# A perceiver layer: keys and queries turned by VectorE in 32x32 blocks, and scores on 16 parts of the array

## What is computed

```python
x = x + xattn(layernorm(x), ctx)      # 16 heads of 32: softmax(q k^T / sqrt(32)) v with k = v = ctx, then @ W_out.T + b_out
x = x + attn(layernorm(x))            # projections, rope, 16 heads over the 32 rows of a batch, then @ Wo + bo
x = x + ffn(layernorm(x))             # softmax gate over 8 experts, argmax; that expert's gelu MLP 512-512-512
```

## Time and profile before

| | us |
|---|---|
| median of 3 runs | 944.97 |
| lowest and highest | 943.59, 949.37 |
| profiled execution | 948.28 |
| its span, first to last instruction | 946.1 |

### The profile page before, as it was taken

The page is one execution under the profiler, slowest core; times in us unless marked ns, Lnnn a source line. Parts: engine busy times, 40 slices in busy tenths (PEclk is TensorE's granted clock), DMA queues, the critical chain, the costliest instruction groups (busy, mean ns, idle before and its releaser), DMA issues.

```text
span 946.1 us, 27317 instructions
## 1 busy us (share of the span) xinstructions
PE 853.3 (90%) x11224; PEld 644.3 (68%) x11224; DVE 523.7 (55%) x1127; ACT 436.3 (46%) x1083; POOL 314.5 (33%) x661
## 2 busy tenths in 40 slices
PE   5997989999999999999999999999976459999998
PEld 3554767767686776868777686777765347777775
DVE  2565456565656656566665656656543343554552
ACT  2444455555645555464555646455532123343332
POOL 2022323233332323232332423233231045666553
PEclk9998999999999999999999999999987569999999
DMA  9512121112212112122212212211050189433330
GB/s 316 185 47 58 46 78 60 58 60 78 69 58 80 57 58 84 55 69 70 68 58 66 82 54 65 77 58 58 2 189 12 42 280 387 130 94 99 111 93 3
DMA packets 40074, 85.40 MB, mean 90 GB/s; under 512 B 9230, under 2 KB 10510, under 8 KB 39952
## 3 DMA queue, kind: packets, MB, share of 16 engines
q1 hardware_dynamic: 34048, 71.58, 23.1%
q0 software_dynamic: 3680, 10.23, 3.2%
q10 hardware_dynamic: 2224, 1.86, 0.7%
HBM read 75.27 MB, written 10.22 MB: 90 GB/s over the span
## 4 chain that ended last, share of the span: by engine, by line
PE 72%; DVE 9%; ACT 8%; issue 6%; POOL 3%; ACTq 1%; DMA 0%; DVEq 0%; POOLq 0%
PE bank L414 9%; PE scores L1351 9%; PE bank L1366 8%; PE bank L416 7%; PE bank L415 7%; PE scores L459 6%; PE bank L472 4%; PE bank L447 4%; PE bank L408 3%; PE bank L485 3%; ACT soft_block L764 3%; ACT prob L717 2%; DVE negmax L919 2%; POOL operand_lo L1156 2%; PE bank L623 2%
## 5 line engine op out<-in xcount | busy, mean ns | idle before, releaser
L717 ACT ACTIVATE prob<-scores,negmax 128x257 f32<-128x257 f32 x256 | 119.3, 472 | 161.9 <-DVE negmax L919 160.9
L919 DVE TENSOR_REDUCE negmax<-scores 128x2 f32<-128x514 f32 x128 | 88.2, 689 | 151.4 <-PE scores L459 151.4
L414 PE MATMUL bank<-qkv_hi,operand_hi 128*128 128x396 f32 x256 | 103.0, 402 | 0.0
L1351 PEld LDWEIGHTS scores<-rows_t,w 128*128 128x128 f32 x736 | 87.7, 196 | 11.6 <-issue 10.5
L415 PE MATMUL bank<-qkv_lo,operand_hi 128*128 128x396 f32 x256 | 88.9, 347 | 0.0
L416 PE MATMUL bank<-qkv_hi,operand_lo 128*128 128x396 f32 x256 | 88.8, 347 | 0.0
L459 PE MATMUL scores<-k_t,q_t 32*32 32x257 f32 x2048 | 86.9, 395 | 1.9 <-ACT prob L717 0.5
L1351 PE MATMUL scores<-rows_t,w 128*128 128x128 f32 x736 | 87.9, 279 | 0.7 <-ACT rows_t L1389 0.7
L447 PE MATMUL bank<-consts,context 128*128 128x128 f32 x512 | 79.7, 279 | 4.5 <-ACT k_t L702 4.4
L1366 PE MATMUL bank<-w_all,hidden 128*128 x184 | 82.8, 592 | 0.0
L472 PE MATMUL bank<-consts,prob 128*128 128x128 f32 x512 | 81.1, 281 | 0.0
(11 more groups left out here) (211 smaller groups left out, 1744.0 us busy)
## 6 DMA issues: line engine op xcount, KB each, us to landing
context<-in_ctx SPq DMA_DIRECT2D x64, 512.0 KB, 3.8
w_all<-in_L_ffn_W SPq DMA_DIRECT2D x16, 1024.0 KB, 8.3
b<-in_L_ffn_b SPq DMA_DIRECT2D x23, 256.0 KB
x_tile<-in_x SPq DMA_DIRECT2D x16, 256.0 KB, 3.8
x_scratch<-x_tile SPq DMA_DIRECT2D x16, 256.0 KB, 2.0
soft_block<-in_L_xattn_W_out SPq DMA_DIRECT2D x1, 1024.0 KB, 12.1
late<-in_L_attn_Wk_r_w SPq DMA_DIRECT2D x1, 1024.0 KB, 14.4
soft_block<-in_L_attn_Wo_w SPq DMA_DIRECT2D x1, 1024.0 KB, 5.1
```

What stands on the lines that cost most here:

```text
L414: pe.matmul(to, op_hi[op][:, c, :], w_hi[name][:, c, columns], start=(c == 0), stop=False)
L717: act.activation(prob[pair][:, gg, :], scores[:, gg, 0:J], ACT.Exp, bias=negmax[b % 2][:, g:g + 1], accum_out=sums[t % 2][:, g, bl:bl + 1] ...
L919: dve.tensor_reduce(negmax[b % 2][:, 2 * pair:2 * pair + 2], scores[:, :, 0:J], AX.X, ALU.max, negate=True).then_inc(maxed, 1)
L1351: done = pe.matmul(scores[:, m // 2, (m % 2) * P:(m % 2 + 1) * P], w1[h * G + k][:, m * P:(m + 1) * P], rows_t[h][:, k, :], start=(k == 0) ...
```

## The change

- Keys: PE's transposes, the copies and POOL's work for the last row go. DVE turns each half of a batch's context (`turn_keys`, two block transposes of 128x512) in 32x32 blocks from SBUF to SBUF, at steps 1 and 3 of the batch before. So a quarter of the context rows stays on each 32 partitions, with a head's channels across them.
- Queries: DVE turns a tile's normed rows once the same way (`turn_queries`). Four DMAs per batch on SP's queue then copy the batch's 32 partitions to each of the four partition quarters (`spread_queries`). The scale goes into the norm's root.
- Scores: one block per batch. 16 matmuls of one column for the 257th row, then 64 matmuls of 64 columns, each on 32 rows and 32 columns of the array: row quarter `r` writes bank `r`, head `hl` its quarter of the output partitions. `scores` has four banks. `largest` is one reduction over 1024 elements and two tiny operations; `exp` reads 256 elements across four banks; `exp_last` makes the last row's probabilities on ACT.
- Banks: of eight, four go to scores, one to probabilities and one to attention, so the tile's stages and the set-up's units have two instead of three.
- Steps: nearly all offsets move, and `move_prob` is ACT's for both pairs.

```diff
+QK = C2 * HD
...
 TILE = BT * STEPS
 (INVERT, PLACE_LAST, PLACE_INV, X_BIAS, SPREAD, SPREAD_INV, ATT, ATT_INV, ATT_HI, ATT_LO, XOUT, X1, SCALE1, TURN1, QKV, OUT_BIAS, TURN_Q, TURN_K,
  SELF, SOFT, SOFT_EXP, SOFT_SUM, SOFT_SCALE, SOFT_TURN, SOFT_PLACE, AV, OUT, X2, SCALE3, TURN3, GATE, CHOOSE, RANK) = (
-    -7, -1, -5, 3, 0, 4, 2, 4, 8, 5, 10, 14, 15, 19, 23, 25, 34, 39, 43, 45, 47, 49, 49, 55, 55, 60, 83, 87, 87, 96, 110, 113, 119)
-
-MEASURE_X, SCALE_X = 2 * STEPS + 6, 2 * STEPS + 10
+    -8, 3, -7, 11, 0, 4, 2, 5, 3, 9, 12, 19, 21, 22, 27, 40, 37, 39, 48, 54, 54, 55, 58, 60, 58, 70, 88, 92, 97, 99, 117, 118, 130)
+
+MEASURE_X, SCALE_X = 2 * STEPS + 1, 2 * STEPS + 6
 LAST_STEP = TILE * T + RANK + 2
 
 
-SCORE_AT = (0, 4)
-TURN_C_AT = (2, 7)
-TURN_P_AT = (5, 10)
-ATTEND_AT = (10, 15)
-KEEP_AT = (4, 10)
-QUERIES_AT = 10
-
-DVE_KEYS = (1,)
-DVE_PROB = (0,)
+
+SCORE_AT = 0
+KEYS_AT = (1, 3)
+TURN_P_AT = (3, 10)
+ATTEND_AT = (6, 11)
+QUERIES_AT = 34
+SPREAD_Q_AT = 0
+
+DVE_PROB = ()
 
 
...
-UNIT_AT = [2, 3, 4, 6, 8, 10, 11, 13, 14, 15, 16, 17, 18, 20, 22, 23, 25, 27, 29, 31, 33, 35, 36, 37, 39]
+UNIT_AT = (2, 4, 4, 6, 6, 8, 9, 9, 14, 16, 17, 17, 17, 21, 22, 24, 25, 25, 25, 30, 35, 35, 36, 37, 42)
...
-    negmax = [sba(f"negmax{i}", [P, G]) for i in range(2)]
+    negmax_256, negmax, last_s = sba("negmax_256", [P, G]), sba("negmax", [P, G]), sba("last_s", [P, G])
...
-    k_t = [sbx(f"k_t{i}", [P, 2, J]) for i in range(2)]
-    prob = [sbx(f"prob{i}", [P, 2, J]) for i in range(2)]
+    k_t = [sbx(f"k_t{i}", [P, C2, D]) for i in range(2)]
+    prob = sbx("prob", [P, G, C2, P])
     prob_t = [sbx(f"prob_t{i}", [P, 2, C2, P]) for i in range(2)]
-    q_t = sbx("q_t", [P, G, BT, S])
+    q_t = sbx("q_t", [P, D])
+    staged_c = sbx("staged_c", [P, G, D])
+    q_all = [sbx("q_all0", [P, D]), staged_c[:, 3, :]]
 
     low_bias = sba("low_bias", [P, G])
     rot_bias = sba("rot_bias", [P, 2, 2, ROPE])
     rot_q, rot_k = sba("rot_q", [P, 2, 2, ROPE]), sba("rot_k", [P, G, 2, ROPE])
...
-    scores = ctx.enter_context(nc.psum_tensor("scores", [P, 2, 512], F32))
-    psum = [ctx.enter_context(nc.psum_tensor(f"bank{i}", [P, 512], F32)) for i in range(6)]
...
         return s_[:, :].unsqueeze(2).broadcast_to([P, H, S])
+
+    def quarter_of(b, r):
+
+        bl = b % BT
+        return q_all[b % 2][r * HD:(r + 1) * HD, :], q_t[bl * HD:(bl + 1) * HD, :]
 
...
-    bank_of = {"spread": 0, "xout": 1, "norm": 2, "qkv0": 0, "qkv2": 0, "out": 0, "inv": 1, "gate": 1, "av": 1, "qkv1": 1, "q": 1, "k": 1, "norm3": 2, "rank": 2, "qkv3": 2, "self": 2}
+    bank_of = {"spread": 1, "xout": 1, "norm": 1, "qkv0": 1, "qkv2": 1, "out": 0, "inv": 0, "gate": 0, "av": 0, "qkv1": 0, "q": 0, "k": 1, "norm3": 0, "rank": 1, "qkv3": 0, "self": 1}
...
 
+        def spread_queries(b):
+
+            until.wait_ge(queries_turned, b // BT + 1)
+            until.wait_ge(scored, b - 1)
+            if b == 1:
+                until.wait_ge(columns_made, ROT_Q)
+            for r in range(4):
+                sp.dma_start(*quarter_of(b, r)).then_inc(queries_spread[b % 2], 16)
+
         def load_x(t):
+            if t >= 2:
+                until.wait_ge(unit_done, UNITS.index(("rot", 0)) + 1)
...
@@ -372,6 +391,8 @@
         for step in range(LAST_STEP):
             b, k = divmod(step, STEPS)
             t, bl = divmod(b, BT)
+            if k == SPREAD_Q_AT and b + 1 < B:
+                spread_queries(b + 1)
             if k == 5 and bl == 1 and t + 1 < T:
...
-        def place_queries(t):
-            until.wait_ge(const_loaded, 16)
-            until.wait_ge(normed_x, t + 1)
-            if t:
-                until.wait_ge(k_moved[1], BT * t + 1)
-            turn(norm_x, context_bank, queries_turned)
-
-        def turn_context(b, pair):
-            until.wait_ge(context_loaded[b % 4], 16 * (b // 4 + 1))
-
-            if pair == 0:
-                until.wait_ge(k_moved[1], b)
-                if b <= 1 or b % BT == 1:
-                    until.wait_ge(queries_placed, b // BT + 1)
-            else:
-                until.wait_ge(k_moved[0], b + 1)
-            for gg in range(2):
-                for c in range(C2):
-                    g = 2 * pair + gg
-                    at = (gg * C2 + c) * P
-                    done = pe.transpose(context_bank[:, at:at + P], context[b % 4][:, c, g * P:(g + 1) * P], ident)
-            done.then_inc(context_turned, 1)
-
-        def score(b, pair):
-            t, bl = divmod(b, BT)
-            until.wait_ge(queries_placed, t + 1)
-            until.wait_ge(k_moved[pair], b + 1)
-            until.wait_ge(k_last_moved, 2 * b + pair + 1)
-            until.wait_ge(exped, 4 * b + 2 * pair)
-            for hl in range(HL):
-                for gg in range(2):
-                    rows, place = slice(hl * HD, (hl + 1) * HD), hl ^ (2 * pair + gg)
-                    done = pe.matmul(scores[place * S:(place + 1) * S, gg, 0:J], q_t[rows, 2 * pair + gg, bl, :],
-                                     k_t[pair][rows, gg, :], start=True, stop=True)
+        def score(b):
+            quarter, column = divmod(b, HD)
+            until.wait_ge(last_q_made, 1)
+            until.wait_ge(queries_spread[b % 2], 64 * (b // 2 + 1))
+            until.wait_ge(exped, G * b)
+            until.wait_ge(keys_turned, 2 * b + 2)
+
...
+            rows = slice(quarter * HD, (quarter + 1) * HD)
+            for g in range(G):
+                for hl in range(HL):
+                    at = (g * HL + hl) * HD
+                    pe.matmul(scores[hl * S:(hl + 1) * S, quarter, G * QK + g:G * QK + g + 1], q_all[b % 2][rows, at:at + S],
+                              last_q[rows, at + column:at + column + 1], start=True, stop=True)
+            for g in range(G):
+                for r in range(4):
+                    rows = slice(r * HD, (r + 1) * HD)
+                    for hl in range(HL):
+                        at = (g * HL + hl) * HD
+                        done = pe.matmul(scores[hl * S:(hl + 1) * S, r, g * QK:(g + 1) * QK], q_all[b % 2][rows, at:at + S],
+                                         k_t[b % 2][rows, :, at:at + HD], start=True, stop=True)
             done.then_inc(scored, 1)
 
...
-                                         prob_t[pair][:, gg, c, place * S:(place + 1) * S], start=(c == 0), stop=(c == C2 - 1))
+                                         prob_t[pair][:, gg, c, hl * S:(hl + 1) * S], start=(c == 0), stop=(c == C2 - 1))
             done.then_inc(attended, 1)
 
         def set_up(n):
             kind, c = UNITS[n]
-            bank = banks[n % 3]
-            if n >= 3:
-                until.wait_ge(*emptied_unit(n - 3))
+            bank = banks[n % 2]
+            if n >= 2:
+                until.wait_ge(*emptied_unit(n - 2))
             else:
                 until.wait_ge(last_ready, 1)
             if kind == "xout":
...
         def exp(b, g):
-            pair, gg = divmod(g, 2)
-            until.wait_ge(maxed, 2 * b + pair + 1)
             t, bl = divmod(b, BT)
-            if gg == 0:
-                until.wait_ge(prob_turned, 2 * (b - 1) + pair + 1)
-                until.wait_ge(plast_kept, 2 * (b - 1) + pair + 1)
-                until.wait_ge(inverted, t - 1)
-            act.activation(prob[pair][:, gg, :], scores[:, gg, 0:J], ACT.Exp, bias=negmax[b % 2][:, g:g + 1],
+            until.wait_ge(maxed, b + 1)
+            until.wait_ge(prob_turned, 2 * (b - 1) + g // 2 + 1)
+            until.wait_ge(inverted, t - 1)
+            act.activation(prob[:, g, :, :].rearrange("p c (r k) -> p r c k", r=4),
+                           scores[:, :, g * QK:(g + 1) * QK].rearrange("p r (c k) -> p r c k", c=C2), ACT.Exp, bias=negmax[:, g:g + 1],
                            accum_out=sums[t % 2][:, g, bl:bl + 1]).then_inc(exped, 1)
+
+        def exp_last(b):
+            t, bl = divmod(b, BT)
+            until.wait_ge(maxed, b + 1)
+            until.wait_ge(plast_placed, t - 1)
+            until.wait_ge(inverted, t - 1)
+            act.activation(plast[t % 2][:, :, bl], last_s[:, :], ACT.Exp).then_inc(plast_kept, 1)
...
             return t_.rearrange("p (q a c) -> p q a c", q=2, a=2)
 
-        def move_keys(b, pair):
-            until.wait_ge(context_turned, 2 * b + pair + 1)
-            if b:
-                until.wait_ge(scored, 2 * b - 1 + pair)
-            dve.tensor_copy(k_t[pair][:, :, 0:C2 * P], context_bank[:, :].rearrange("p (g n) -> p g n", g=2)).then_inc(k_moved[pair], 1)
+        def turn_queries(t):
+            until.wait_ge(normed_x, t + 1)
+            for i in range(2):
+                until.wait_ge(queries_spread[i], 64 * 2 * t)
+            dve.transpose(q_t[:, :], norm_x[:, :]).then_inc(queries_turned, 1)
+
+        def turn_keys(b, c):
+            until.wait_ge(context_loaded[b % 4], 16 * (b // 4 + 1))
+            until.wait_ge(scored, b - 1)
+            dve.transpose(k_t[b % 2][:, c, :], context[b % 4][:, c, :]).then_inc(keys_turned, 1)
 
```

(43 more changed lines are left out.)

123 lines of the change are left out of this document (41 added, 82 removed).

## The result

The changed kernel takes 1065.73 us, the median of 4 executions (1063.68 to 1069.39), where the kernel before, measured beside it, takes 944.28 (943.26 to 949.37). The ratio is 1.128, with a 95% interval from 1.123 to 1.133. The forecast was 936 us and its range ended at 974, so both the direction and the range were wrong. Medians leave out an execution that took over 1.5% longer than the fastest of its kernel.

A forecast was written before the change was run, and what follows sets the result against it. PE's instruction order, its work plus waits, was taken as the bound. A tile went from 41.0 to 40.5 us; 15 distances gave -7.5, set-up -2, drain 0: 944.97 - 9.5 = 935.5, stated as 936, range 903 to 974.

The forecast's parts named there:

- 160 x 8 ns = 1.3 us, and with the tail 1.4: PE's score block: 160 records at 8 ns each, 1.4 us a block; below 1.2, above 2.0.
- narrow windows: Short trace stretches of the kernel before: 8 score records begin within 0.06 us, 13 attend records within 0.12.
- 0.4 a tile, bounds 0 and 3.4: Clock falling to half after batch 2's thin stretch, 5.4 us with 2.25 of work: 0.4 us a tile.
- the forecast 40.5: Tile time: 41.0 - 3.7 PE work + 2.8 more waits + 0.4 clock = 40.5 us.
- Forecast 5.8 us a tile: PE's waits over a tile's four batches, longest 3.1 in batch 2: 5.8 us against 3.0 before.
- waits covered: Rival: most waits covered, 1.2 more instead of 2.8, no clock fall; 38.5 a tile, 905 us; chance 0.22.
- -2 forecast: Set-up: 4 us of transposes go, three rotating banks become two; -2 us, bounds -6 and +6.
- stay hidden: Queries' four DMAs per batch, 256 KB, issued 10 us ahead, against 3.8 us for a 512 KB context load.
- 0 forecast: Drain, a chain through the same stages: 0 us, bounds -3 and +5.
- 958: Clock rival: half-clock stretch after batch 2's gap every tile, 42.0 a tile, deciding from 41.8; 958 us, chance 0.20.
- 972: Rival: score records 12.2 ns apart, blocks of 2.0 us, 42.9 a tile; 972 us, chance 0.10.
- 1115: Rival: floor under matmul starts, 27 ns a record, score block 4.4 us, 12.0 more a tile; 1115 us, chance 0.03.

The follow-up runs named there:

- kernel with 64 records: Changed kernel with 16 score matmuls of 256 columns a batch for 64 of 64, some scores wrong: 64 records a block, not 160; 922.1 us, ratio 0.975.
- two banks: Kernel before with the set-up's units on two rotating banks instead of three, the stages keeping three: 946.7 us, ratio 1.001.
- kernel cut in four: Kernel before with each score matmul of 257 columns cut into four pieces of columns, 128 records a batch instead of 32: 964.5 us, ratio 1.018.

## Why the prediction was wrong, point by point

**The score block: mis-sized, and the wrong limit.** The step was "160 x 8 ns = 1.3 us, and with the tail 1.4". The undisturbed block takes 1.64, 10.2 ns a record, inside the bounds of 1.2 and 2.0, and that costs 1.0 us a tile. The failing part is what the step took for granted: that 160 records follow each other as 8 or 13 do. The narrow windows show starts of instructions that were already there. In the kernel before no 256 instructions in a row took under 6.27 us, so nothing in its trace could show what a dense block of 320 would do. It held a hint, though: 16 KB packets of an instruction queue, 89 of them, each of which began about 1.0 us into a line (median of 67), and a span with 11224 matmul records and as many weight loads. The sum of instructions over the block, 320, was in the text only as 160 records. The weight loads were left out. In the runs no engine was waited for there: holes at the seams of the instruction stream cost 5.7 us a tile in all (3.05 in scores, 2.05 in attend, 0.6 in dense products).

**The clock: 0.4 a tile, bounds 0 and 3.4.** The mechanism, a thin stretch and half clock behind it, was right, and the rows above show it: after 2.23 us of busy time in 3.40 with a hole in it the next stretch ran at 0.50, the 1.2 GHz level. The place was not. I looked for it behind batch 2's scores; it comes behind holes, anywhere. 10.7 us at half clock can cost at most 5.3. An estimate by what is left over is 4.1: the forecast 40.5, and 1.0 for the block, 5.7 for the holes, less 2.8 for waits that came out smaller, make 44.4; 3.7 more remain to 48.1, beside the 0.4 that was in.

**The waits: too large, on the safe side.** Forecast 5.8 us a tile. Measured from start to start, before the probabilities' transposes 2.19 us, before SPREAD_INV 1.09 (1.17 from 419.71 to 420.88, of which 0.23 is the usual distance; the forecast said 0.8, measured is 0.9), before TURN stages 0.1: about 3 in all without the usual distances, as before the change. Where holes delay PE, other engines catch up, so this tile is a poor witness. The kernel with 64 records is a better one. Its waits, in the rows above, come to about 4.7 us a tile without the usual distances, 1.9 more than before the change. The forecast had 2.8 more and the rival "waits covered" 1.2, so the truth lay between. By batches they are 1.1, 0.5, 2.3 and 0.9 us where the forecast had 0.8, 1.1, 3.1 and 0.8. Batch 2 was rightly the longest, but only 0.3 of its wait stands before QKV; 1.0 stands before attend. Its tile of 38.3 is close to that rival's 38.5, in part by luck: its score blocks take 5.06 us a tile, where the forecast's 5.6 are in the 38.5.

**What held.** The reduction of 1024 elements was put at 1.22 us and took 1.225. Block transposes took 690 ns against 702. VectorE has 27.4 us in a tile against 27, ScalarE 21.7 against 22, and neither binds. The transposes of context are gone from PE, 3.6 us a tile.

**The set-up: -2 forecast, +14.4 measured, outside its bounds.** The step said that the queries' DMAs "stay hidden" and "only the first batch pays, a few us". In the waits of PE before the first SPREAD stand:

```profile
PE bank L641 <- DMA soft<-in_ctx: 7.9, 1, 7.9
PE scores L458 <- DMA q_all<-q_t: 6.9, 1, 6.9
```

The first score block starts at 15.4 us instead of 11.4, behind loads that keep the DMA engines 90% busy; the second at 39.7 instead of 27.8. The cases tell some of it apart: two banks 2.0 us; the later first block 4.0; and 10.2 us at half clock before the first SPREAD where it was 3.4, which costs at most 3.4 more. If these add, some 5 stay open. With 64 records a block the first SPREAD comes at 80.4, so 5.0 hang on the number of records, though not by holes: none stands inside a score or attend block of the set-up. The error was to carry over an average landing time from the steady part to a stretch where the DMA share is twice as high.

**The drain: 0 forecast, +2.1 measured,** inside its bounds.

**The rivals.** The slower ones were 958, 972 and 1115. The first's threshold of 41.8 a tile was passed, but not by its mechanism. The last came nearest in time and had 0.03, for a floor under starts that isn't there: 160 records began within 1.64 us, 10.2 ns apart, and in the kernel cut in four an added record cost 4.5 ns. The rule of the Trainium skill, "TensorE: Matmul & The Clock Gate", section "Wait — 56ns, not 53.3ns?", of 25 ns between starts doesn't hold for matmuls on different parts of the array; a kernel that stays at 10.2 ns a record still loses, by the instruction stream. No rival was about the supply of instructions, which is the real gap: 68% more matmul records were counted for the distance between their starts and for nothing else.

**Could the design win?** With the supply solved and everything else as it is, the tile would be the 38.3 us of the 64-record kernel and 1.5 for the further starts (6.56 us of scores against 5.06), 39.8, and the whole about 922 + 16 x 1.5 = 946 us: no gain, since the set-up has taken what the tiles give. That is an estimate, not a run. No kernel here that computes everything was faster than the one before.

## What to carry to other kernels

Count PE's instructions, weight loads too, and look at the densest 256 in a row, not only at the sum: here a line of 256 that PE could do in under 2.7 us was mostly stretched to about 3.5, and half clock followed on many of the pauses. Cutting matmuls into small pieces was cheap where dense work spread them (4.5 ns a record in blocks of 128 instructions), and ruinous in one long block. A pause that ends on "issue" in the middle of a block without waits is the sign; the instruction queue's packets and the distance between pauses in instructions confirm it.

## What the runs showed of the hardware

- PE's instructions come in packets of 16 KB, 256 instructions. The packet for the next line began 0.9 us (median of 34) after PE had begun on the line before it. PE resumed 2.6 us after the packet began (median of 32; 2.3 to 2.75), with or without bulk transfers in the steady part, and the packet itself takes about 1.1 us.
- Lines with a hole behind them lasted 3.46 us with it (median). A line of 2.92 us in the kernel cut in four had no hole; under 2.7 us, 34 of 38 had one in the changed kernel. Short lines passed without one where their packet had begun earlier, from 1.3 us ahead of the line's start to 0.1 us behind it.
- Matmul records on different 32x32 parts of the array started 10.2 ns apart over 160 of them.
- The same kernel, shifted by one and by half a line, took 1055 and 1074 us (two executions each). The tile is alike, 47.1 and 47.2 us; the difference is in the set-up, 85.7 and 99.5 us to the first SPREAD, with five holes in the second.
